# Clearing the message sums on two engines, and a drain of GpSimd's queue ahead of the last results

## The reference, cut to what matters

```
x0, x1 = split(layernorm(x));  y0, y1 = x0 @ lin1_w0, x1 @ lin1_w1
w = silu(edge_scalars @ fc_w1) @ fc_w2          # 4 groups of 64 per edge
mids = concat(w_a*y0[src]*ea0, w_b*(y1[src].ea1), w_c*y0[src]*ea1, w_d*ea0*y1[src])   # 512 per edge
agg = segment_sum(mids, dst)                    # 512 per node
x = x + (products of x and of agg with small matrices)
```

## Time and profile before

| what | value |
|---|---|
| time, median of 3 runs | 2090.07 us (2084.49 to 2091.8) |
| the profiled execution's own time | 2092.74 us |
| its span | 2091.0 us |
| PE busy | 1781.2 us (85%) |
| DVE busy | 1159.5 us (55%) |
| POOL busy | 1019.1 us (49%) |
| ACT busy | 981.2 us (47%) |
| `msg` phase in the span | about 1157 to 1711 us |
| `last` phase in the span | about 1933 to 2091 us |

### The profile page before, as it was taken

The page is one execution under the profiler, slowest core; times in us unless marked ns, Lnnn a source line. Parts: engine busy times, 40 slices in busy tenths (PEclk is TensorE's granted clock), DMA queues, the critical chain, the costliest instruction groups (busy, mean ns, idle before and its releaser), DMA issues. The chain is left out here.

```text
span 2091.0 us, 37517 instructions
## 1 busy us (share of the span) xinstructions
PE 1781.2 (85%) x9925; PEld 1450.6 (69%) x9925; DVE 1159.5 (55%) x2786; ACT 981.2 (47%) x2962; POOL 1019.1 (49%) x1048
## 2 busy tenths in 40 slices
PE   2699998998779836999936599999999988995898
PEld 1466665665446625999924599999999877664787
DVE  6333333333321575444456799999999974434121
ACT  3355544444123611333226577777777743441221
POOL 2677777777700003555500677777777730000443
PEclk7799999999879756999967799999999999997899
DMA  9677777777500125999961577777777733553553
GB/s 234 184 237 238 233 231 235 229 235 231 168 16 0 38 68 185 353 350 350 341 155 50 181 216 220 219 218 221 220 214 220 214 115 83 168 159 101 185 177 104
DMA packets 246154, 397.04 MB, mean 190 GB/s; under 512 B 66177, under 2 KB 133314, under 8 KB 245712
## 3 DMA queue, kind: packets, MB, share of 16 engines
q1 hardware_dynamic: 193276, 241.84, 37.3%
q0 software_dynamic: 52224, 150.15, 23.7%
q10 hardware_dynamic: 462, 2.76, 0.6%
HBM read 298.20 MB, written 97.44 MB: 189 GB/s over the span
## 5 line engine op out<-in xcount | busy, mean ns | idle before, releaser
L1739 POOL DMA_INDIRECT msg_got<-y_dram,block_src x416 | 415.0, 998 | 226.8 <-issue 107.0
L1756 ACT ACTIVATE msg_scaled<-msg_plain,msg_w 128x125 f32<-128x125 f32 x1392 | 416.0, 386 | 131.8 <-DVE msg_plain L1786 121.7
L657 POOL DMA_INDIRECT sum_got<-xn_dram,block_src x416 | 393.6, 946 | 138.3 <-issue 112.4
L1777 PEld LDWEIGHTS msg_ps_z<-msg_prod,msg_scaled 128*125 128x125 f32 x2784 | 341.7, 188 | 13.2
L1777 PE MATMUL msg_ps_z<-msg_prod,msg_scaled 128*125 128x128 f32 x2784 | 343.1, 273 | 0.0
L703 PEld LDWEIGHTS sum_ps_sum<-sum_got,sum_onehot 128*125 128x125 f32 x928 | 176.7, 196 | 189.7 <-issue 174.5
L703 PE MATMUL sum_ps_sum<-sum_got,sum_onehot 128*125 x928 | 255.2, 400 | 50.9 <-POOLq L651 48.6
L763 DVE TENSOR_TENSOR agg<-sum_ps_sum,agg 125x256 f32 x232 | 98.5, 424 | 314.5 <-PE sum_ps_sum L703 312.7
L1773 PE MATMUL msg_ps_z<-msg_prod,msg_plain 128*125 128x256 f32 x928 | 247.4, 389 | 19.6 <-DVE msg_prod L1805 17.3
L734 ACT ACTIVATE sum_wide<-sum_ps_w,sum_rec 128x128 f32<-128x128 f32 x416 | 130.4, 364 | 232.1 <-PE sum_ps_w L688 232.1
L1805 DVE TENSOR_TENSOR msg_prod<-msg_w,msg_got 128x384 f32<-128x384 f32 x464 | 236.0, 548 | 0.0
(11 more groups left out here) (321 smaller groups left out, 2405.3 us busy)
## 6 DMA issues: line engine op xcount, KB each, us to landing
ffn_run_w<-in_L_ffn_w SPq DMA_DIRECT2D x128, 512.0 KB, 6.0
msg_w<-edge_w SPq DMA_DIRECT2D x232, 260.0 KB, 3.6
edge_w<-sum_wide SPq DMA_DIRECT2D x52, 1040.0 KB, 5.1
ffn_rows<-route_hrow SPq DMA_DIRECT2D x25, 448.0 KB
wd<-in_L_ffn_Wd SPq DMA_DIRECT2D x8, 1024.0 KB
sum_got<-xn_dram,block_src POOLq DMA_INDIRECT x416, 3.6
msg_got<-y_dram,block_src POOLq DMA_INDIRECT x416, 3.6
table_got<-ffn_results SPq DMA_DIRECT2D x10, 560.0 KB
```

The source lines that it names most:

```text
L657: pool.indirect_dma_start(got[:, (b + 1) % RING, u, :], None, k.xn_dram, bass.IndirectOffsetOnAxis(ap=k.block_src[:, b, u:u + 1].bitcast(U ...
L1739: pool.indirect_dma_start(got[:, (b + 1) % RING, u, :, :].rearrange("p k v -> p (k v)"), None, k.y_dram, bass.IndirectOffsetOnAxis(ap=k.bl ...
L1756: last = act.activation(scaled[s % MB][:, x, c, :], plain[s % MB][:, c, :], ACT.Copy, scale=w[:, s % RS, c, D + x:D + x + 1])
L1777: last = pe.matmul(z[0:P, 4:6 + x:1 + x, :], by[:, x, c, :], p[:, c, 4 + x:8:3 - x, :], start=False, stop=(x == 2 and u == KC - 1), skip_g ...
```

## The change

The clearing of `agg` is split: VectorE clears tiles 0 to 11 (12 x 512 values) as its first work of the phase, ahead of the first mask, and ScalarE writes tiles 12 to 24 (13 x 512 values) by a copy scaled by 0 of a broadcast column, ahead of its first scaling. A new semaphore `rest_zero` is waited for once, ahead of the first `add_sum`. In the last phase GpSimd's queue has a `drain` in front of the send of block 28 of 0 to 31.

```diff
@@ sum_messages
-        ps_lanes, lanes_made = ph.ps("lanes", [128, P]), ph.sem("lanes_made")
+        ps_lanes, lanes_made, rest_zero = ph.ps("lanes", [128, P]), ph.sem("lanes_made"), ph.sem("rest_zero")
@@ block.scalar
+            rest = k.agg[:, T // 2:T, :].rearrange("p t d -> p (t d)")
+            act.activation(rest, k.ident[:, 0:1].to_broadcast([128, (T - T // 2) * 2 * D]), ACT.Copy, scale=0.0).then_inc(rest_zero, 1)
             for s in range(NST):
@@ add_sum
                 dve.wait_ge(added, 1 + n)
+                if n == 0:
+                    dve.wait_ge(rest_zero, 1)
@@ block.vector
             dve.wait_ge(lanes_made, 1)
+            dve.memset(k.agg[:, 0:T // 2, :], 0.0).then_inc(added, 1)
             mask(0)
-            dve.memset(k.agg[:, :, :], 0.0).then_inc(added, 1)
@@ run_second_experts, block.gpsimd
                     fetch(n + LEAD)
+                if n == m.blocks - 4:
+                    pool.drain()
                 send(n)
```

## The result

The changed kernel takes 2084.8 us (median of 20 runs, 2076.37 to 2089.78) against 2090.35 us for the kernel before in the same sessions; the ratio is 0.9969 with a 95% interval of 0.9960 to 0.9978, 6.5 us less (4.6 to 8.4); the two medians are 5.6 us apart. 5.7 us had been forecast, and the range of 2079 to 2090 us holds the time. By the ratio the gain lies a hair beyond the 0.3% that was called the limit of what can be told, on the side given 0.33; by the medians it lies a hair within. The profiled execution has a span of 2078.5 us, 12.5 us less than before's. Of these, 7.4 us lie in the two phases that the change touches and 5.1 us in the others, as scatter, so I compare the two phases and not the spans.

The account below looks back on a forecast made before the run. GpSimd's gathers were taken to bound the second half of `msg`, and its final drain to cost 5.28 us at the end. From the median, 2090.07 - 5.7 (5.1 drain, 0.6 gather pace) = 2084.4 us; whole range 2079 to 2090 us.

Parts of the forecast that it names:

- VectorE's half: Start of `msg`: clearing 12 of 25 tiles takes 5.15 us, first multiplication 5.4 to 6.2 us earlier.
- ScalarE's half: Start of `msg`: ScalarE's clear of 6656 values takes 5.8 us, bounds 4.5 and 10 us, at cost 0.
- the cover: Start of `msg`: ScalarE's idle wait for the factors, 10.05 us until 1163.44, hides its half of the clear.
- The lead is worth nothing, GpSimd sets the end: `msg`: VectorE's 5.4 to 6.2 us of lead finds no gathered blocks; the last arrival sets the end, worth 0.
- The pace of the gathers: `msg`: gathers come closer where VectorE waits, 0.9 us gained, 0.3 lost; net gain 0.6 us, bounds 0 and 2.2.
- the rule of whole multiplications: `msg`: five newly uncovered gathers could each lose a whole multiplication of 0.55 us, 2.7 us in place of 0.3.
- one of the signs: `msg`: last arrival 540 to 541 us behind the third gather; arrivals ending over 3 us earlier or later count as wrong.
- The drain: Last phase: drain ahead of send 28 leaves 0.2 us of the final drain's 5.28 us, a gain of 5.1 us.
- a drain that stays: Rival, last phase: only 1.2 us of the final drain go, 1.8 us with `msg`, 2088.3 us; chance 0.20.
- The drain's cover: Last phase: the new drain takes about 5 us, send 28 goes some 2 us late, the next on time; cost 0.
- all of the clear comes through: Rival, `msg`: GpSimd's pace follows VectorE's, so `msg` gives 5.5 us, 2079.5 us in all; chance 0.10.
- The worse rhythm: Rival, GpSimd's 416 gathers in `msg`: one in five long, not one in seven, costs 7.5 us, 2092.5 us; chance 0.06.

Follow-up runs that it names:

- the late gathers: Changed kernel with a memset of 128 x 5632 values on GpSimd ahead of the first gather; ratio to before 0.9982, message phase 557.9 us.
- the slow session: Changed kernel plus a drain in `ffn0_run` and `sum`'s last four arrivals counted by SyncE, run once more while both kernels ran a fifth slower; ratio 0.9972.
- the whole clear: Changed kernel with the clear whole on VectorE again, as its first work, none on ScalarE; ratio to before 0.9967, message phase 554.3 us.
- the clear alone: Changed kernel without its drain ahead of send 28; 2088.32 us, ratio to before 0.9979, message phase 551.8 us.
- the changed kernel run again: Changed kernel, nothing altered, measured in another session for comparison; ratio to before 0.9945, message phase 551.6 us.
- the drain at 31: Changed kernel with its drain in front of the last send, 31, in place of 28; last phase 3.9 us longer than the changed kernel's.

## Why the prediction was right, step by step

- *VectorE's half, ScalarE's half, the cover*: rows of 5.18 and 5.75 us against 5.15 and 5.8; ScalarE was done at 1158.9, 2.1 us ahead of the mask for which its first scaling waited. Right. The first multiplication came 6.7 us earlier, not 5.4 to 6.2. The step took the 2.62 us without a releaser for something that may move or go; they are part of the `memset` and shrink with it, so that VectorE was ready 6.9 us earlier, about when the second arrival was counted (1161.5). From there the arrival is the limit: in the other kernels with the split clear the first multiplication stands 8.1 to 8.6 us behind the first gather (without the late gathers and the slow session), 6.0 to 6.5 us earlier than before.
- *The lead is worth nothing, GpSimd sets the end*: right. The last step waits the same 0.46 us, and the late gathers and the whole clear show it from both sides.
- *The pace of the gathers*: right in sign, too small. 0.6 us forecast, 2.1 in the pair of profiles, 1.5 in the mean of all; the bound of 2.2 held. The 0.3 us set against it for gathers that lose the memset's cover was the smaller part: the twelfth gather starts 0.1 us later behind the first than before (0.2 us with the clear alone, 0.6 us in the changed kernel run again), and nothing like the 2.7 us by the rule of whole multiplications was seen. What I mis-sized is the pace: 1.299 us in place of 1.301 for the first part, and 1.298 in place of 1.301 behind it, where I had forecast no gain. For the same reason one of the signs failed: the last arrival was to come 540 to 541 us behind the third gather and came 538.8 us behind it (1695.26 - 1156.41), 2.1 us earlier than before, where over 3 us was to count as wrong.
- *The semaphore*: right, no further barrier appeared.
- *The drain*: 4.9 us of 5.1, with 0.38 us left where I took 0.2. The upper of my two prices for a DMA, 82 ns, is the true one in this phase. The reasoning behind the step was weaker than its number: the 20 ns for each DMA that I read from three other drains is no law. 208 gathers cost what 416 do, so the agreement of 416 and 128 says nothing of a cost for each DMA. Nor had I read all drains: those of two phases without indirect DMAs, at 48.6 and 756.9 us of the kernel before, take 0.70 and 0.60 us, beside work of GpSimd's own. The chance of 0.20 for a drain that stays was fair: what decided was a regularity of the last phase that no row of before showed alone.
- *The drain's cover*: right. Send 28 was late, the next on time.
- *The rivals*: a drain that stays is excluded, and with it the idea that sends that move nothing carry the surplus. That all of the clear comes through is excluded by the whole clear and by the late gathers. The worse rhythm didn't come; it became a better one.
- *The range of the likeliest case*: 2090.07 - 4.9 + 1 is 2086.2 us, not the 2087 us that I gave; nothing hangs on it.

## What to carry to other kernels

A queue's drain at a barrier is work, not only waiting, and the chain of waits doesn't list it; look for the gap between the last DMA and the end of the span, then for the sequencer's drain in it. A drain a few DMAs ahead of the end takes that work away if the queue idles there for long enough, costs its full length where the queue is the bound (9.1 us in `sum`), and costs what exceeds the queue's idle time where what it delays is the last item (the drain at 31). And an engine that starts earlier gains nothing if another has set the pace by the end: follow the lead over the phase, from its size at the start to its size at the end, before the start is improved.

## What the runs showed of the hardware that was not expected

The long gathers are not strewn about. In the kernel before 51 of 54 begin some 0.97 to 1.03 us behind the start of a mask, and the gathers and VectorE's steps keep step, seven to two:

```profile
1301.45 0.67 DVE L1786 TENSOR_TENSOR msg_plain<-msg_ps_lanes,pair_dst 128x500 f32<-128x500 f32 x1
...
1302.46 1.27 POOL L1739 DMA_INDIRECT msg_got<-y_dram,block_src  x1 [0.30 <-issue]
...
1310.59 0.67 DVE L1786 TENSOR_TENSOR msg_plain<-msg_ps_lanes,pair_dst 128x500 f32<-128x500 f32 x1
...
1311.61 1.27 POOL L1739 DMA_INDIRECT msg_got<-y_dram,block_src  x1 [0.30 <-issue]
```

Both times 1.01 to 1.02 us after the mask's start, beside the first multiplications. In the changed kernel, where VectorE waits, 43 gathers are long and not 54; each costs 0.31 us more than the usual one, and some others are lengthened by less. That the waiting breaks the step is what this suggests; no run tried it by itself. In the kernel before 229 gathers start beside a multiplication and 54 of them are long, so that two SBUF inputs alone are not what lengthens one. Which access collides was not tried.

Two things on drains stay open: why one costs 8.55 us behind 208 gathers and behind 416 and only 2.51 behind 128 DMAs of `ffn0_run`, and what exactly it waits for behind a fetch in flight.
